# First attention: x in two parts, context laid out turned, mask product in 64x64 pieces

## The chip, the cores and the metric

The kernel runs on one core of a Trainium2 chip. Its engines work side by side, each through its own queue of instructions in order: TensorE (PE, matmuls; PEld, its weight loads), VectorE (DVE), ScalarE (ACT), GpSimd (POOL), and SyncE (SP), which issues most of the loads. They wait for one another with semaphores. The metric is the time of one execution on the device in microseconds (us), lower is better.

## The reference

Four layers, each a gated cross attention and a gated feed-forward block, are applied to x (16 batches of 128 rows of 256 values, float32). The change touches the first attention alone:

```python
x = x + jnp.tanh(g_xattn[0]) * _L0_xattn_ref(_layernorm(x), ctx, ctx, mask, wq, wk, wv, wo, bo)

def _L0_xattn_ref(q, k, v, mask, wq, wk, wv, wo, bo):     # 16 heads of 16 values
    qh, kh, vh = heads(q @ wq), heads(k @ wk), heads(v @ wv)
    scores = einsum('nqha,nkha->nhqk', qh, kh)
    scores = where(mask == 0, -1e10, scores)
    attn = softmax(scores / sqrt(16), axis=-1)
    return einsum('nhqk,nkha->nqha', attn, vh).reshape(N, Lq, 256) @ wo + bo
```

The layer normalisation takes mean and variance over the 256 values of each row of x. ctx is 16 x 128 x 256, the mask 16 x 1 x 128 x 128 of int32.

## The kernel before, in words

All of x stays in on-chip memory for the whole program. The first stage is `narrow_attention` (L291), one pass over the 16 batches, written out by hand for every engine; the later stages are not touched.

**Start.** `Prologue` (L178) holds the loads and the statistics that come before the loop. SyncE issues four loads of x (`on_sync`, L189, four batches of 512 KB in each), then ctx and mask of batches 0 and 1, then wq, wk, wv, wo and the bias bo (L334 to L342). VectorE takes `bn_stats` of the 16 batches, each four after their load (`on_vector`, L218), waits for the tanh of the gates, and `finish_norm_vector` (L229) turns the statistics into 1/std and -mean/std in a chain of eight small operations, with a square root on ScalarE (`finish_norm_scalar`, L258) in the middle. TensorE meanwhile runs ten `stay_warm` products (L265, two matmuls each) on the identity.

**A batch.** `front` (L386) has three fillings of one PSUM bank: T turns the normalised x (L393) and ctx (L396) with two transposes each, and ScalarE evicts the four as one tile xcT (L512); QK makes Q and K from it in 16 matmuls (L402), V makes V in 4 (L407). `scores` (L411) first writes the additive mask into four score banks, each by one matmul of a 128x128 bf16 identity against the mask repeated for four heads (512 columns, L418), and then adds the scores of the 16 heads, 32 matmuls with tiles of 32 rows (L425). VectorE (`shift`, L589) takes the row maximum of each bank (L593) and subtracts it (L597); ScalarE takes the exponential (L534); TensorE turns the probabilities (`transposed`, L435); `weighted` multiplies them with V and with ones (L449, tiles of 32 columns); VectorE divides (L604, L608); `project` multiplies with wo (L458), and VectorE adds the result into x and takes its statistics (L615, L284). `weigh` (L583) makes the additive mask of a batch from the int32 mask (L586).

**Order.** Each engine's `body` runs one batch and takes in parts of its neighbours: TensorE does scores of batch b, the last turning of b-1, the projection of b-2, QK of b+1, the weighted sum of b-1, V of b+1, three turnings of b, T of b+2. `over_batches` (L53) writes out the first two and the last two bodies and loops over pairs of the others, with one branch a pair. Waits in the loop compare a semaphore with a count worked out in a register. SyncE loads ctx and mask of batch b when T of b-2 is filled and the mask of b-2 is used (L346 to L350). GpSimd adds the gated bias to x (L376).

## Time and profile before

| | |
|---|---|
| median of 3 runs | 1626.53 us (1624.03 to 1630.96) |
| span of the profiled execution, first to last instruction | 1600.8 us |
| median less that span | 25.7 us |
| mean granted TensorE clock over the span | 0.923 of full |
| TensorE busy, matmuls / weight loads | 1386.6 us (87%) / 1150.0 us (72%) |
| VectorE, ScalarE, GpSimd busy | 953.2, 664.8, 422.6 us |
| first attention, up to the first instruction of the next stage | 195.8 us |

The profile is of one execution. Times in it are in us from the start of the span. "Idle before" is the time for which the engine stood still before an instruction, and behind the arrow stands what ended it; "issue" means that it waited for nothing that the profile shows. The granted clock is the share of TensorE's full 2.4 GHz that the chip allows in a stretch; its lower level is 0.50.

### The profile page before, as it was taken

How to read it: one execution, taken by the hardware profiler on the slowest of the kernel's cores; microseconds unless marked ns; L12 is line 12 of the kernel's file. 1: busy time of each engine (PE TensorE's matmuls, PEld its weight loads, DVE VectorE, ACT ScalarE, POOL GpSimd, SP SyncE). 2: the span in 40 equal slices, each digit the busy share in tenths (PEclk: the TensorE clock that was granted, in tenths of full speed). 3: DMA queues.
4: the chain of work that ended last, by engine and by line, in shares of the span. 5: the costliest groups of instructions: out<-in, count | busy, mean ns of one | idle time of the engine just before them, and what ended most of it. 6: DMA issues, size and time to landing. Idle time of an engine off the chain costs nothing. (4 is left out here: it accounts for less than half of the span.)

```text
span 1600.8 us, 31601 instructions
## 1 busy us (share of the span) xinstructions
PE 1386.6 (87%) x10662; PEld 1150.0 (72%) x10662; DVE 953.2 (60%) x2331; ACT 664.8 (42%) x1313; POOL 422.6 (26%) x578
## 2 busy tenths in 40 slices
PE   8999878889999994999999998999999997401588
PEld 5888645677799983788888887779999996400245
DVE  4888665666422225777777774832222265688887
ACT  3666453420344430333333334335555522430277
POOL 1000000012122210122221221246666633421141
PEclk9999999899799997999999998889999999755799
DMA  3000020673111107111111202012333344421001
GB/s 107 21 20 15 6 92 1 218 268 61 60 34 41 34 22 226 62 51 49 49 47 32 44 1 93 1 52 92 92 93 93 86 173 134 108 19 10 1 14 40
DMA packets 105328, 106.53 MB, mean 67 GB/s; under 512 B 36080, under 2 KB 92160, under 8 KB 105088
## 3 DMA queue, kind: packets, MB, share of 16 engines
q1 hardware_dynamic: 89312, 70.91, 14.6%
q0 software_dynamic: 11136, 28.93, 6.6%
q10 hardware_dynamic: 4768, 5.25, 1.1%
q8 instruction: 64, 1.05, 0.3%
q14 instruction: 48, 0.39, 0.1%
HBM read 83.19 MB, written 20.71 MB: 65 GB/s over the span
## 5 line engine op out<-in xcount | busy, mean ns | idle before, releaser
L3598 PEld LDWEIGHTS L2f_bank<-L2f_xT,L2f_w_tile 128*128 128x128 f32 x1264 | 154.5, 193 | 7.4 <-ACT L2f_xT L3662 3.4
L3598 PE MATMUL L2f_bank<-L2f_xT,L2f_w_tile 128*128 128x128 f32 x1264 | 155.2, 276 | 3.0 <-ACT L2f_xT L3662 3.0
L785 POOL TENSOR_TENSOR L2x_probs<-L2x_probs,L2x_inv_sum 128x512 f32<-128x512 f32 x64 | 66.3, 1057 | 268.4 <-DVE L2x_inv_sum L1062 268.4
L3712 DVE TENSOR_TENSOR L2f_hT<-L2f_gate_h,L2f_bank 128x256 f32<-128x256 f32 x79 | 33.3, 421 | 148.5 <-ACT L2f_gate_h L3669 148.5
L3521 POOL DMA_INDIRECT L2f_y_rows<-L2f_xn,L2f_put_row x79 | 78.2, 989 | 55.2 <-DVE L2f_xn L3728 51.6
L3656 ACT COPY L2f_w_tile<-L2f_w_up 128x1024 f32 x79 | 82.7, 1046 | 17.4 <-issue 17.4
L3513 POOL DMA_INDIRECT L2f_rows<-L2f_x_rows,L2f_take_row x79 | 77.0, 975 | 44.7 <-DVE L2f_take_row L3496 21.3
L3598 PEld LDWEIGHTS L1f_bank<-L1f_xT,L1f_w_tile 128*128 128x128 f32 x736 | 85.6, 192 | 1.1
L3598 PE MATMUL L1f_bank<-L1f_xT,L1f_w_tile 128*128 128x128 f32 x736 | 85.9, 275 | 0.0
L3615 PE MATMUL L1f_bank<-L1f_w_down,L1f_hT 128*128 x368 | 83.1, 379 | 0.0
L3615 PE MATMUL L2f_bank<-L2f_w_down,L2f_hT 128*128 x316 | 81.4, 380 | 0.1
L3615 PEld LDWEIGHTS L1f_bank<-L1f_w_down,L1f_hT 128*128 128x128 f32 x368 | 68.2, 190 | 8.4
L3573 DVE TENSOR_SCALAR L1f_hT<-L1f_bank,expert_b 128x128 f32<-128x128 f32 x92 | 25.9, 344 | 77.6 <-PE L1f_bank L3598 77.6
L829 PE MATMUL L2x_bank<-L2x_wv,L2x_xcT 128*128 128x512 f32 x128 | 63.3, 617 | 2.4 <-issue 1.0
L836 PE MATMUL L2x_bank<-L2x_xcT,L2x_wq 128*128 128x128 f32 x512 | 62.6, 275 | 1.8 <-DMA L2x_wq<-in_L_xattn_Wq 1.8
L836 PE MATMUL L2x_bank<-L2x_xcT,L2x_wk 128*128 128x128 f32 x512 | 62.5, 275 | 1.3 <-DMA L2x_wk<-in_L_xattn_Wk 1.3
L836 PEld LDWEIGHTS L2x_bank<-L2x_xcT,L2x_wq 128*128 128x128 f32 x512 | 60.8, 192 | 3.6 <-DMA L2x_wq<-in_L_xattn_Wq 2.6
L3571 ACT ACTIVATE L1f_hT<-L1f_bank,expert_b 128x128 f32<-128x128 f32 x92 | 26.4, 368 | 88.3 <-PE L1f_bank L3598 88.3
L3290 PEld LDWEIGHTS L2f_bank<-L2f_xT_all,sh_gu 128*128 128x128 f32 x512 | 61.4, 197 | 0.7
L3669 ACT ACTIVATE L2f_gate_h<-L2f_bank 128x256 f32<-128x256 f32 x79 | 30.3, 384 | 75.6 <-PE L2f_bank L3598 75.6
L3290 PE MATMUL L2f_bank<-L2f_xT_all,sh_gu 128*128 128x128 f32 x512 | 61.4, 280 | 0.0
L836 PEld LDWEIGHTS L2x_bank<-L2x_xcT,L2x_wk 128*128 128x128 f32 x512 | 59.7, 192 | 2.1 <-DMA L2x_wk<-in_L_xattn_Wk 2.1
(677 smaller groups left out, 3321.2 us busy)
## 6 DMA issues: line engine op xcount, KB each, us to landing
L1f_w_up<-in_L_ffn_w SPq DMA_DIRECT2D x16, 512.0 KB, 8.2
L1f_w_down<-in_L_ffn_w SPq DMA_DIRECT2D x16, 512.0 KB, 9.0
L2f_got<-L2f_y_rows SPq DMA_DIRECT2D x16, 512.0 KB, 4.4
L2f_w_up<-in_L_ffn_gate_w SPq DMA_DIRECT2D x16, 256.0 KB, 2.9
L2f_w_up<-in_L_ffn_up_w SPq DMA_DIRECT2D x16, 256.0 KB, 3.0
L2f_w_down<-in_L_ffn_down_w SPq DMA_DIRECT2D x16, 256.0 KB, 3.6
x<-in_x SPq DMA_DIRECT2D x4, 512.0 KB, 7.9
L0x_ctx<-in_ctx SPq DMA_DIRECT2D x16, 128.0 KB, 2.1
```

Source lines behind the costliest of these rows:

```text
L785: nc.gpsimd.tensor_tensor(probs[c][:, :, :], probs[c][:, :, :], inv_sum[:, c, :][:, :, None].to_broadcast([P, 4, P]), ALU.mult).then_inc(s ...
L829: last = nc.tensor.matmul(dst[:, :], xcT[j][:, KT + k, :], wv[:, k, half * 512:(half + 1) * 512], start=(k == 0), stop=(k == KT - 1))
L836: last = nc.tensor.matmul(dst[:, i * P:(i + 1) * P], w[:, k, t * P:(t + 1) * P], xcT[j][:, of + k, :], start=(k == 0), stop=(k == KT - 1))
L3290: t = nc.tensor.matmul(bank[2 + 2 * j + u][:, f * P:(f + 1) * P], sh_gu[:, u, k, f * P:(f + 1) * P], xT_of(b)[:, k * P:(k + 1) * P], start ...
L3513: pool.indirect_dma_start(out=rows[t % 4][:, :], out_offset=None, in_=x_dram[:, :], in_offset=bass.IndirectOffsetOnAxis(ap=take_row[:, t:t ...
L3521: pool.indirect_dma_start(out=y_dram[:, :], out_offset=bass.IndirectOffsetOnAxis(ap=put_row[:, t:t + 1], axis=0), in_=y[t % 4][:, :], in_o ...
L3571: x = nc.scalar.activation(dst, products(j, m), ACT.Relu, bias=bias_col)
L3598: x = nc.tensor.matmul(products(j, m), w_tile[j][:, at:at + P], xT[j][:, k * P:(k + 1) * P], start=(k == 0), stop=(k == KT - 1))
L3615: x = nc.tensor.matmul(bank[6 + j][:, 0:D], hT[j][:, k * P:(k + 1) * P], cols(w_down, e * (FT * D) + k * D, D), start=(k == 0), stop=(k == ...
L3656: nc.scalar.copy(w_tile[j][:, 0:KT * UP], cols(w_up, e * (KT * UP), KT * UP)).then_inc(q["w_tile"], 1)
L3669: nc.scalar.activation(gate_h[j][:, 0:F], bank[2 + j][:, 0:F], ACT.Silu).then_inc(q["silu"], 1)
L3712: nc.vector.tensor_tensor(hT[j][:, 0:F], gate_h[j][:, 0:F], bank[2 + j][:, F:2 * F], ALU.mult).then_inc(q["h"], 1)
```

## The change

- **x in two parts.** SyncE loads the first chunk of x (batches 0 to 3), then wq, wk, the inputs of batch 0, wv, the other three chunks, the inputs of batch 1, wo. VectorE takes the statistics of batches 0 to 3 and finishes their normalisation, makes the first two normalised tiles and the first mask, and does the same for batches 4 to 15 before the second mask. `finish_norm_vector` and `finish_norm_scalar` run twice, on a range of batches. ScalarE takes the tanh of the gates behind the second square root, loads the bias through its own queue, and VectorE makes the gated bias at the end of its first body.
- **Context turned.** The host passes ctx a second time, with each batch transposed into two 128x128 tiles. SyncE loads those; T turns only x, and its eviction is of 256 columns. The wait for ctx moves from T to QK, and SyncE's wait from T of b-2 to V of b-2.
- **Mask product in pieces.** The int32 mask of a batch is loaded twice, into the two halves of the partitions (two loads of 64 partitions), and `weigh` makes 256 columns of it. For two banks at a time, TensorE waits for both, increments a semaphore of its own (`settle`), and writes four pieces, each a 64x64 part of the identity against 512 columns: two halves of a bank's partitions for each of the two halves of the array's rows, each half of the rows into a bank of its own. Eight pieces take the place of four matmuls.
- Seven warming products instead of ten.

```diff
-            prologue.on_sync(sp)
-            for b in range(2):
-                load_inputs(b, b)
-            for n in ("wq", "wk", "wv", "wo"):
-                sp.dma_start(w[n][:, :, :], ins[L0_X[n]].rearrange("(k p) n -> p k n", p=P)
-                             ).then_inc(s["w_" + n[1]], 16)
-            sp.dma_start(bo[:, :], ins[L0_X["bo"]].rearrange("(a n) -> a n", a=1).to_broadcast([P, D])
-                         ).then_inc(s["w_o"], 16)
+            prologue.load_x(sp, (0,))
+            load_weight("wq")
+            load_weight("wk")
+            load_inputs(0, 0)
+            load_weight("wv")
+            prologue.load_x(sp, (1, 2, 3))
+            load_inputs(1, 1)
+            load_weight("wo")
             def body(j, b):
 
-                sp.wait_ge(s["filled"], (b - 2) * NF + (T + 1))
+                sp.wait_ge(s["filled"], (b - 2) * NF + (V + 1))
...
             def load_inputs(j, b):
-                sp.dma_start(ctx_in[j][:, :], one(ins["ctx_1024"], b)).then_inc(s[f"ctx_in{j}"], 16)
-                sp.dma_start(mask_in[j][:, :], one(ins["mask_Bx1xSxS2_ik1"].rearrange("b a q k -> b (a q) k"), b)
-                             ).then_inc(s[f"mask_in{j}"], 16)
+                sp.dma_start(ctxT[j][:, :, :].rearrange("p t c -> p (t c)"), one(ins["ctx_turned"], b)
+                             ).then_inc(s[f"ctxT{j}"], 16)
+                for r in range(MS):
+                    sp.dma_start(mask_in[j][r * MW:(r + 1) * MW, :, :],
+                                 one(ins["mask_Bx1xSxS2_ik1"].rearrange("b a q k -> b (a q) k"), b
+                                     ).rearrange("(c p) k -> p c k", p=MW)).then_inc(s[f"mask_in{j}"], 16)
...
                 if f == T:
 
                     pe.wait_ge(s["xn"], b + 1)
-                    pe.wait_ge(s[f"ctx_in{j}"], loads(b, j))
                     for k in range(KT):
-                        nc.tensor.transpose(front_bank[:, k * P:(k + 1) * P], xn[j][:, k * P:(k + 1) * P],
-                                            core.ident[:, :])
-                    for k in range(KT):
-                        last = nc.tensor.transpose(front_bank[:, (KT + k) * P:(KT + k + 1) * P],
-                                                   ctx_in[j][:, k * P:(k + 1) * P], core.ident[:, :])
+                        last = nc.tensor.transpose(front_bank[:, k * P:(k + 1) * P], xn[j][:, k * P:(k + 1) * P],
+                                                   core.ident[:, :])
                 elif f == QK:
-                    for n, of, at in (("wq", 0, 0), ("wk", KT, D)):
+
+                    pe.wait_ge(s[f"ctxT{j}"], loads(b, j))
+                    for n, of, at in (("wq", xT, 0), ("wk", ctxT, D)):
...
-                for i in range(4):
-
-                    after(pe, s["shifted"], b * 4 + (i - 3))
-                    nc.tensor.matmul(score_bank[i][:, :].rearrange("p (h k) -> p h k", h=4), mask_diag[:, :],
-                                     mask_add[j][:, None, :].to_broadcast([P, 4, P]), start=True, stop=False)
+                for i0 in range(0, 4, MS):
+
+                    after(pe, s["shifted"], b * 4 + (i0 + MS - 4))
+                    settle(pe, s["pe_passed"])
+                    for c in range(MS):
+                        for r in range(MS):
+                            rows = slice(r * MW, (r + 1) * MW)
+                            nc.tensor.matmul(score_bank[i0 + r][c * MW:(c + 1) * MW, :
+                                                                ].rearrange("p (h k) -> p h k", h=4),
+                                             mask_diag[rows, rows],
+                                             mask_add[j][rows, c, None, :].to_broadcast([MW, 4, P]),
+                                             start=True, stop=False)
...
-            stay_warm(core, out_bank, 10)
+            stay_warm(core, out_bank, 7)
...
-            prologue.on_scalar(act)
-            finish_norm_scalar(core, act, s, temps)
+            prologue.load_gates(act)
+            act.dma_start(bo[:, :], ins[L0_X["bo"]].rearrange("(a n) -> a n", a=1).to_broadcast([P, D])
+                          ).then_inc(s["b_o"], 16)
+            nc.scalar.preload_act_table(ACT.Sqrt)
+            finish_norm_scalar(core, act, s, temps, 0, FIRST)
             take(0, 0, T)
...
             take(0, 0, V)
             take(1, 1, T)
+            finish_norm_scalar(core, act, s, temps, FIRST, B, before=1)
+            prologue.squash_gates(act)
             over_batches(act, body)
...
                 if not two_left(b):
                     weigh(j, b + 2)
+                if first:
+
+                    dve.wait_ge(prologue.sems["gates"], 1)
+                    dve.wait_ge(s["b_o"], 16)
+                    nc.vector.tensor_scalar(gated_bias[:, :], bo[:, :], core.gate(layer, 0), None, ALU.mult
+                                            ).then_inc(s["gated_bias"], 1)
...
-            prologue.on_vector(dve)
-            dve.wait_ge(prologue.sems["gates"], 1)
-            finish_norm_vector(core, dve, s, temps)
+            prologue.stats(dve, 0, FIRST)
+            finish_norm_vector(core, dve, s, temps, 0, FIRST)
             norm(0, 0)
             norm(1, 1)
             weigh(0, 0)
+            prologue.stats(dve, FIRST, B)
+            finish_norm_vector(core, dve, s, temps, FIRST, B, before=1)
             weigh(1, 1)
-
-            dve.wait_ge(s["w_o"], 32)
-            nc.vector.tensor_scalar(gated_bias[:, :], bo[:, :], core.gate(layer, 0), None, ALU.mult
-                                    ).then_inc(s["gated_bias"], 1)
```

## Rows read from the trace of the kernel before

**Rows 1.** Busy time by stretch: PE, PEld, DVE, ACT, POOL, granted clock, DMA share, GB/s.

```profile
12.62:15.38 2.76, 0.01 (x1) 0.03 (x1) 2.43 (x13) 0.22 (x1) 0.00 (x0) 1.00 0.74 239
...
16.78:20.18 3.40, 3.40 (x16) 3.21 (x16) 0.07 (x1) 0.00 (x0) 2.02 (x3) 0.57 0.22 58
20.18:23.21 3.03, 1.10 (x5) 0.68 (x5) 0.00 (x0) 1.54 (x5) 0.00 (x0) 0.98 0.00 0
23.21:25.96 2.75, 2.75 (x8) 1.31 (x8) 0.00 (x0) 1.58 (x2) 0.00 (x0) 0.50 0.08 24
...
80.00:100.00 20.00, 19.92 (x288) 16.69 (x286) 17.27 (x29) 12.54 (x28) 1.45 (x2) 1.00 0.06 20
```

**Rows 2.** Timeline 0 to 40: start, duration, engine, line, operation, tiles [idle before].

```profile
7.19 1.41 DVE L223 BATCH_NORM_STATS2 stats<-x 128x6 f32<-128x256 f32 x4 [5.33 <-DMA x<-in_x]
...
8.77 4.43 DVE L223 BATCH_NORM_STATS2 stats<-x 128x6 f32<-128x256 f32 x12 [0.16 <-DMA x<-in_x]
...
11.18 0.19 PEld L270 LDWEIGHTS L0x_bank<-ident 128*128 128x128 f32 x1 [0.24 <-issue]
11.61 0.19 PEld L270 LDWEIGHTS L0x_bank<-ident 128*128 128x128 f32 x1 [0.24 <-issue]
13.23 0.19 DVE L237 TENSOR_TENSOR L0x_temps<-stats 128x16 f32<-128x16 f32 x1
...
14.71 0.74 DVE L279 TENSOR_SCALAR L0x_xn<-x,rstd,neg_mean_rstd 128x256 f32<-128x256 f32 x2
...
15.38 0.41 PE L393 MATMUL L0x_bank<-ident,L0x_xn 128*128 128x128 f32 x2 [2.76 <-DVE L0x_xn L279]
...
16.05 0.59 ACT L512 COPY L0x_xcT<-L0x_bank 128x512 f32<-128x512 f32 x1 [1.87 <-PE L0x_bank L396]
...
21.02 0.37 ACT L520 COPY L0x_kT<-L0x_bank 128x256 f32<-128x256 f32 x1
...
27.40 0.69 DVE L593 TENSOR_REDUCE L0x_top<-L0x_bank 128x4 f32<-128x512 f32 x1 [10.54 <-PE L0x_bank L425]
```

**Rows 3.** Issue of wk in the same timeline; then the loads: size, us to landing.

```profile
7.81 0.65 SPq L339 DMA_DIRECT2D L0x_wk<-in_L_xattn_wk  x1
...
L0x_wk<-in_L_xattn_wk SPq DMA_DIRECT2D x1, 256.0 KB, 6.6
```

**Rows 4.** Timeline of TensorE in the loop (PEld: its weight loads).

```profile
82.84 1.03 PE L418 MATMUL L0x_bank<-L0x_mask_add,L0x_mask_diag 128*128 128x512 bf16 x4
...
92.66 0.38 PE L396 MATMUL L0x_bank<-ident,L0x_ctx 128*128 128x128 f32 x2
92.88 1.03 PE L418 MATMUL L0x_bank<-L0x_mask_add,L0x_mask_diag 128*128 128x512 bf16 x4
93.84 1.17 PE L425 MATMUL L0x_bank<-L0x_kT,L0x_qT 32*128 32x128 f32 x32
...
103.17 0.55 PEld L418 LDWEIGHTS L0x_bank<-L0x_mask_add,L0x_mask_diag 128*128 128x128 bf16 x4 [0.34 <-issue]
```

**Rows 5.** Timeline of VectorE in the same stretch.

```profile
93.64 0.21 DVE L586 TENSOR_SCALAR L0x_mask_add<-L0x_mask 128x128 bf16<-128x128 int32 x1
93.88 0.41 DVE L279 TENSOR_SCALAR L0x_xn<-x,rstd,neg_mean_rstd 128x256 f32 x1
95.03 0.69 DVE L593 TENSOR_REDUCE L0x_top<-L0x_bank 128x4 f32<-128x512 f32 x1 [0.73 <-PE L0x_bank L425]
```

**Rows 6.** Timeline of TensorE in the third attention, where tiles of half size stand.

```profile
740.19 1.95 PE L836 MATMUL L2x_bank<-L2x_xcT,L2x_wq 128*128 128x128 f32 x16
741.97 1.95 PE L836 MATMUL L2x_bank<-L2x_xcT,L2x_wk 128*128 128x128 f32 x16
...
745.95 1.09 PE L875 MATMUL L2x_bank<-L2x_probsT,L2x_v 128*64 128x128 f32 x16
746.97 1.16 PE L847 MATMUL L2x_bank<-L2x_kT,L2x_qT 64*128 64x128 f32 x16
748.06 1.98 PE L829 MATMUL L2x_bank<-L2x_wv,L2x_xcT 128*128 128x512 f32 x4
```

More of the change, by code:

```diff
@@ L188, in __init__, with load_x @@
                                                                                    "cleared"])
-    def on_sync(self, sp):
+    def load_x(self, sp, chunks):
         core = self.core
-        for i in range(B // self.CHUNK):
+        for i in chunks:
             b = i * self.CHUNK
@@ L216, in on_gpsimd, with stats @@
                                      ).then_inc(s["cleared"], 1)
-    def on_vector(self, dve):
-        for b in range(B):
+    def stats(self, dve, lo, hi):
+        for b in range(lo, hi):
             if b % self.CHUNK == 0:
@@ L224, in on_vector, with finish_norm_vector @@
                                          ).then_inc(self.sems["stats"], 1)
-        dve.wait_ge(self.sems["stats"], B)
-def finish_norm_vector(core, dve, s, temps):
+        dve.wait_ge(self.sems["stats"], hi)
+NORM_STEPS = 7
+def finish_norm_vector(core, dve, s, temps, lo=0, hi=B, before=0):
     nc = core.nc
-    st = core.stats[:, :].rearrange("p (b k) -> p b k", k=6)
+    done = before * NORM_STEPS
+    st = core.stats[:, 6 * lo:6 * hi].rearrange("p (b k) -> p b k", k=6)
     mean_e, var_e, mean_o, var_o = st[:, :, 1], st[:, :, 2], st[:, :, 4], st[:, :, 5]
-    half, var, mean, root = (temps[:, k, :] for k in range(4))
+    half, var, mean, root = (temps[:, k, lo:hi] for k in range(4))
@@ L247, in finish_norm_vector @@
     nc.vector.tensor_tensor(var, half, var, ALU.add).then_inc(s["norm_var"], 1)
     nc.vector.tensor_tensor(mean, mean_e, mean_o, ALU.add).then_inc(s["norm_step"], 1)
-    dve.wait_ge(s["norm_root"], 1)
-    nc.vector.reciprocal(core.rstd[:, :], root).then_inc(s["norm_step"], 1)
-    dve.wait_ge(s["norm_step"], 6)
-    nc.vector.scalar_tensor_tensor(core.neg_mean_rstd[:, :], mean, -0.5, core.rstd[:, :], ALU.mult, ALU.mult
+    dve.wait_ge(s["norm_root"], before + 1)
+    nc.vector.reciprocal(core.rstd[:, lo:hi], root).then_inc(s["norm_step"], 1)
@@ L255, in finish_norm_vector, with finish_norm_scalar @@
+    dve.wait_ge(s["norm_step"], done + 6)
+    nc.vector.scalar_tensor_tensor(core.neg_mean_rstd[:, lo:hi], mean, -0.5, core.rstd[:, lo:hi], ALU.mult, ALU.mult
                                    ).then_inc(s["norm_step"], 1)
-    dve.wait_ge(s["norm_step"], 7)
-def finish_norm_scalar(core, act, s, temps):
-    act.wait_ge(s["norm_var"], 1)
-    core.nc.scalar.activation(temps[:, 3, :], temps[:, 1, :], ACT.Sqrt).then_inc(s["norm_root"], 1)
+    dve.wait_ge(s["norm_step"], done + 7)
+def finish_norm_scalar(core, act, s, temps, lo=0, hi=B, before=0):
+    act.wait_ge(s["norm_var"], before + 1)
+    core.nc.scalar.activation(temps[:, 3, lo:hi], temps[:, 1, lo:hi], ACT.Sqrt).then_inc(s["norm_root"], 1)
@@ L294, in narrow_attention @@
     NF = 3
+    MS = 2
+    MW = P // MS
     with ExitStack() as ctx:
@@ L303, in narrow_attention @@
         ones32 = sb(f"{tag}_ones32", [P, 2, 32])
-        ctx_in = [sb(f"{tag}_ctx{j}", [P, D]) for j in range(2)]
-        mask_in = [sb(f"{tag}_mask{j}", [P, P], I32) for j in range(2)]
-        mask_add = [sb(f"{tag}_mask_add{j}", [P, P], BF16) for j in range(2)]
+        ctxT = [sb(f"{tag}_ctxT{j}", [P, KT, P]) for j in range(2)]
+        mask_in = [sb(f"{tag}_mask{j}", [P, MS, P], I32) for j in range(2)]
+        mask_add = [sb(f"{tag}_mask_add{j}", [P, MS, P], BF16) for j in range(2)]
         xn = [sb(f"{tag}_xn{j}", [P, D]) for j in range(2)]
-        xcT = [sb(f"{tag}_xcT{j}", [P, 2 * KT, P]) for j in range(2)]
+        xT = [sb(f"{tag}_xT{j}", [P, KT, P]) for j in range(2)]
         qT = [sb(f"{tag}_qT{j}", [P, 2, KT, P]) for j in range(2)]
@@ L582, in weigh @@
             def weigh(j, b):
-                dve.wait_ge(s[f"mask_in{j}"], loads(b, j))
+                dve.wait_ge(s[f"mask_in{j}"], mask_loads(b, j))
                 after(dve, s["scores"], 4 * (b - 1))
-                nc.vector.tensor_scalar(mask_add[j][:, :], mask_in[j][:, :], L0_MASK["compare"], L0_MASK["times"],
+                nc.vector.tensor_scalar(mask_add[j][:, :, :], mask_in[j][:, :, :], L0_MASK["compare"], L0_MASK["times"],
                                         L0_MASK["op"], ALU.mult).then_inc(s["mask_add"], 1)
@@ L3831 @@
     arrays, ins = {}, {}
-    for name in _INS:
-        a = np.ascontiguousarray(inputs[name])
+    turned = np.asarray(inputs["ctx_1024"]).reshape(B, P, KT, P).transpose(0, 3, 2, 1).reshape(B, P, KT * P)
+    for name in _INS + ["ctx_turned"]:
+        a = np.ascontiguousarray(turned if name == "ctx_turned" else inputs[name])
         arrays[f"in_{name}"] = a
```

26 lines of the change are left out of this document (16 added, 10 removed).

## The prediction

> **What bounds the kernel now.** I read the granted clock and the engines' busy shares by stretch first [rows 1], then the order of work from the start of the program to the first softmax [rows 2], the loads behind it [rows 3], and then one turn of the batch loop, TensorE first and VectorE second [rows 4, 5]. The reader is to see two regimes. Up to 27.40 us the kernel is a chain: every engine waits for the one before, and its first link is all of x. In the loop (from the second batch on) TensorE is busy for 19.92 of 20 us and VectorE for 17.27 [rows 1], so TensorE sets the pace. The mask products of two batches stand 10.04 us apart (82.84 to 92.88), across the loop's branch 10.3 us (92.88 to 103.17) [rows 4]. What is left to VectorE is the idle before its first reduction, 0.73 us a batch [rows 5].
>
> **The start.** Before, VectorE takes 16 statistics, from 7.19 until 13.2, then the chain of small operations (13.23 to 14.71, 1.48 us), then the normalised tile of batch 0, and TensorE turns it at 15.38, 0.67 us after 14.71 [rows 2]. After, the first part needs only the four statistics of the first chunk (1.41 us in the same row). The small operations get four columns instead of sixteen, which I take as the same 1.48 us, since they are far below a tile's work. So: 7.19 + 1.41 + 0.03 + 1.48 + 0.67 = 10.78 instead of 15.38.
> From there link by link. Turning x and evicting it took 1.40 us (15.38 to 16.78, where the first Q product starts [rows 1, 2]). Two of the four transposes go (0.22 us, the distance from the turning of ctx to the mask product in [rows 4]) and the eviction is of 256 columns, not 512 (0.37 against 0.59 us [rows 2]): 0.96, to 11.74. The 16 products of Q and K took 3.40 us at a granted clock of 0.57 [rows 1]; 16 of the same shape at full clock take 1.78 us (740.19 to 741.97) [rows 6], with the tail 1.95: to 13.69. From there to the second batch's turning it was 3.03 us at a clock of 0.98, all of it evictions and the product V: to 16.72. Then turning, mask product and scores, 23.21 to 27.40, 4.19 us with the clock at 0.50 for most of it. At full clock they would be 0.27, about 0.65 (below) and 1.19 (93.84 to 95.03 [rows 4, 5]), together 2.1; at half clock some 2.9 with the shorter mask. I take 2.5 in the middle: the first reduction at 19.2 instead of 27.40, a gain of 8.2 us.
> **The clock.** It stood at 0.50 after two stretches of little work: TensorE idle from 12.62 to 15.38, then 1.10 busy of 3.03 us [rows 1]. These are the 2.4 and the 1.2 GHz levels. Seven warming products instead of ten end six matmuls of 0.43 us earlier [rows 2], at 12.62 - 2.6 = 10.0, so the first gap shrinks from 2.76 to 0.7 us; the later one (evictions of Q and K) stays. So Q and K should run fast and a stretch behind them may not. Where it falls into the first loop body, the 16 products of Q and K there cost up to 1.6 us more. I take 0.7 off: **start 7.5 us**, bounds 4.5 (Q and K at half clock, 1.5; mask, scores and first body at half clock, 1.5) and 9.2 (all at full clock, and x a little sooner since less is queued behind it).
> **What moved behind it.** SyncE's queue now has wq, wk, the first inputs and wv ahead of x's chunks 1 to 3. The loads drain as one stream: wk, issued at 7.81, landed 6.6 us later at 14.4 with 2944 KB in front of and in it [rows 3]. After the change wk ends at 1024 KB, where x's second chunk ended (its statistics start at 8.77 [rows 2]), far ahead of 11.74. The last chunk of x ends at 3008 KB, so about 14.6. Its four statistics (1.4) bring VectorE to 16.0, the small operations to about 17.5, but their square root stands on ScalarE behind the eviction of the second batch's turned x (about 17.4), so they end near 18.3 and the second mask (0.35) at 18.65. The scores arrive at 19.2: hidden, with 0.5 us to spare. The tanh of the gates now stands on ScalarE behind that root: a table load of 1.28 us, perhaps a second one before the first exponential, which is due at 19.2 + 1.4 = 20.6. The Trainium skill, ScalarE: Activation LUTs, lists tanh in the set of exp, by which the second load would be absent and nothing is due; no row here shows the pair, and the price otherwise is 0.3 us. The bias load goes to ScalarE's queue, one issue while that engine has nothing to do. The gated bias (0.35 us) goes to the end of VectorE's first body, ahead of 2 us of idle; GpSimd's first additions wait for it, and their first reader is two bodies later.
>
> **The loop.** (a) The turning of ctx goes, 2 matmuls, 0.22 us of TensorE (92.66 to 92.88) [rows 4]. But its cover goes too: at the branch TensorE's queue sat idle 0.34 us before the mask product with nothing left to wait for [rows 4], so there the issuing of instructions is what is late, and the transposes hid part of that. One wait moves out of this place (ctx) and a semaphore increment comes in (twice). I count 0.13 in a body without the branch, 0 in one with it: 0.07 on average.
> (b) The mask product is now 0.96 us from its start to the scores (92.88 to 93.84): four streams of 0.216 (0.86) and 0.10 of bubble, which also stands before other changes of tile size. Eight pieces of 64x64, each of 512 columns still, in two groups of four. No 64x64 piece is in the trace. The nearest rows are pieces of 64 rows by 128 columns and 128 rows by 64 columns: 16 of them in 1.09 and 1.02 us (746.97 to 748.06, 745.95 to 746.97), where 16 of 128x128 take 1.78 [rows 6]. So pieces of two halves of the rows run side by side, and pieces of two halves of the columns too. If both hold at once, four run together: 2 x 0.216 = 0.43, the bubble behind 0.10, a new bubble ahead 0.10, and 0.05 for the second group's weights. That is 0.68, a gain of 0.28. Bounds: 0.35 if the new bubbles are hidden by issuing; a loss of 0.96 if no two of the eight overlap (8 x 0.216 = 1.73, with bubbles 1.93).
> The Trainium skill, TensorEngine Tiling (Array Packing), Key Properties, says that a change of tiling mode drains the engine. The rows agree in kind, 0.10 us before the scores; by it one more change a batch is due, and the sum has it in.
> (c) VectorE makes the mask additive for 256 columns instead of 128: 0.21 us becomes about 0.35, taken between it and the 0.41 of the 256-column operation behind it [rows 5]. Its slack of 0.73 becomes 0.59, more than TensorE wins, so it stays hidden; 0.59 a batch is the most that the loop can give. ScalarE's shorter eviction and SyncE's third issue a batch are off the path: the inputs are asked for two batches ahead.
> Loop: 0.07 + 0.28 = 0.35 a batch, times 15, and 0.28 for the last: **5.5 us**; bounds 9.2 (0.59 each) and a loss of 14.
>
> **Sum.** 7.5 + 5.5 = 13.0 us. The profiled span is 1600.8, the median of the runs 1626.53, so 25.7 lie around the span and do not change. The span goes to about 1588, the time to **1613.5 us**, 0.8% faster. What follows the stage is not touched; it starts earlier, and its clock may switch at other places: 3 us either way, about the distance of the runs shown.
>
> **The rivals.**
> 1. Four pieces do not run together, only pairs (chance 0.14). For it: no row has rows and columns halved together. Against it: each half works alone [rows 6]. Mask 4 x 0.216 + 0.25 = 1.11, a loss of 0.15; loop -0.08 x 16, a loss of 1.3. Time 1626.5 - 6.2 = 1620.
> 2. The start gains little: x's later chunks or the clock hold up the first softmax (0.15). Gain 3 there: 1618.
> 3. **The other side.** The eight pieces run one after the other, each group held by its own increment on TensorE's queue (0.05). The mask takes 1.93 us or, with 0.2 us more for each of the two increments, 2.33: 0.96 to 1.37 more, less 0.07, times 16 = 14 to 21 us, against 7.5 at the start: 1633 to 1640. It decides once the phase before the scores is over 0.5 us longer than now. The rows of halved tiles speak against it.
> 4. Rivals 1 and 2 together (0.05): 1625.
> A rule of the Trainium skill, TensorEngine Tiling (Array Packing), Gotcha 1, is that different row tiles can't use one PSUM bank at once. Here a group's two row halves go to two banks, so it would not force rival 3; the rows of 64 rows each have two banks as well.
>
> **Chances.** Forecast (both gains, 1607 to 1618) 0.61; the rivals as above. A measurement of this kernel can tell about 0.5%, 8.1 us, from no change, so the line is at 1618.4. Faster: 0.58 of the forecast and some 0.10 of rival 2 and 1, 0.68. Same: 0.24. Slower: rival 3 and an unlucky clock, 0.08. The range reaches from the forecast with the loop's ceiling, 1606, to rival 4, 1625.
>
> **What would show it.** In the profile after: the first transpose near 10.8 us and the first reduction near 19.2; starts of neighbouring mask products 9.65 us apart in place of 10.04; mask start to scores start 0.68 us; VectorE's idle before its first reduction 0.2 to 0.3 us. Wrong would be a mask phase over 1 us, a first reduction after 22 us, VectorE without idle, or a later stage that takes back what this one gave.

## The result, and the profile after

The changed kernel takes 1611.51 us (median of 4 runs, 1608.04 to 1620.17), the kernel before 1628.74 (4 runs, 1624.03 to 1631.17): a ratio of 0.9892, interval 0.9858 to 0.9926, some 17 us or 1.1% faster. A second comparison (11 below) gave 0.9895, interval 0.9865 to 0.9925. The forecast was 1613.5 in a range of 1606 to 1625.

The timeline of the changed kernel's start, in the columns of [rows 2]:

```profile
7.31 1.41 DVE L225 BATCH_NORM_STATS2 stats<-x 128x6 f32<-128x256 f32 x4 [5.45 <-DMA x<-in_x]
...
10.63 0.41 PE L411 MATMUL L0x_bank<-ident,L0x_xn 128*128 128x128 f32 x2 [1.21 <-DVE L0x_xn L285]
...
11.07 0.37 ACT L536 COPY L0x_xT<-L0x_bank 128x256 f32<-128x256 f32 x1 [1.45 <-PE L0x_bank L411]
...
11.70 1.13 PE L419 MATMUL L0x_bank<-L0x_xT,L0x_wq 128*128 128x128 f32 x8 [0.66 <-ACT L0x_xT L536]
...
13.83 0.84 ACT L542 ACTIVATE L0x_qT<-L0x_bank,L0x_parity 128x256 f32<-128x256 f32 x2 [2.38 <-PE L0x_bank L419]
...
16.01 1.41 DVE L225 BATCH_NORM_STATS2 stats<-x 128x6 f32<-128x256 f32 x4 [0.26 <-DMA x<-in_x]
...
16.75 0.44 PE L411 MATMUL L0x_bank<-ident,L0x_xn 128*128 128x128 f32 x2 [0.58 <-ACT L0x_v L550]
...
17.68 0.63 PE L439 MATMUL L0x_bank<-L0x_mask_add,L0x_mask_diag 64*64 64x512 bf16 x8 [0.49 <-ACT L0x_xT L536]
...
18.24 1.17 PE L449 MATMUL L0x_bank<-L0x_kT,L0x_qT 32*128 32x128 f32 x32
18.39 1.28 ACT L208 ACT_TABLE_LOAD   x1
...
19.09 0.41 DVE L285 TENSOR_SCALAR L0x_xn<-x,rstd,neg_mean_rstd 128x256 f32<-128x256 f32 x1
...
19.43 0.69 DVE L622 TENSOR_REDUCE L0x_top<-L0x_bank 128x4 f32<-128x512 f32 x1
...
20.88 0.63 ACT L558 ACTIVATE L0x_probs<-L0x_shifted 128x512 f32<-128x512 f32 x1 [0.98 <-DVE L0x_shifted L626]
```

The chain is read as before: first transpose 10.63 instead of 15.38, first Q product 11.70 instead of 16.78, first reduction 19.43 instead of 27.40. The reduction carries no idle in front: VectorE was at work on its normalised tile until then (19.09), and 19.43 is also 1.19 us after the start of the scores, as in the loop: the two are level. Only one table load stands between the second root and the first exponential.

The loop, TensorE first, then VectorE (answers to [rows 4, 5]):

```profile
72.34 0.63 PE L439 MATMUL L0x_bank<-L0x_mask_add,L0x_mask_diag 64*64 64x512 bf16 x8 [0.34 <-issue]
...
81.47 0.38 PE L411 MATMUL L0x_bank<-ident,L0x_xn 128*128 128x128 f32 x2
81.78 0.63 PE L439 MATMUL L0x_bank<-L0x_mask_add,L0x_mask_diag 64*64 64x512 bf16 x8
82.34 1.17 PE L449 MATMUL L0x_bank<-L0x_kT,L0x_qT 32*128 32x128 f32 x32
...
91.66 0.63 PE L439 MATMUL L0x_bank<-L0x_mask_add,L0x_mask_diag 64*64 64x512 bf16 x8 [0.36 <-issue]
...
82.72 0.28 DVE L615 TENSOR_SCALAR L0x_mask_add<-L0x_mask 128x256 bf16<-128x256 int32 x1
82.98 0.41 DVE L285 TENSOR_SCALAR L0x_xn<-x,rstd,neg_mean_rstd 128x256 f32 x1
83.53 0.69 DVE L622 TENSOR_REDUCE L0x_top<-L0x_bank 128x4 f32<-128x512 f32 x1
```

Mask products stand 9.44 us apart (72.34 to 81.78) and, across the branch, 9.88 (81.78 to 91.66), where they stood 10.04 and 10.3 us apart. The mask now takes 0.56 us to the scores (81.78 to 82.34), not 0.96. The wait for issuing at the branch is still there, 0.36 us, and VectorE's idle before its reduction has shrunk from 0.73 to 0.14 us (83.39 to 83.53), too short for the view to name.

Busy time by stretch, the columns of [rows 1]:

```profile
10.00:20.00 10.00, 6.29 (x69) 4.87 (x70) 7.45 (x27) 3.98 (x10) 0.00 (x0) 1.00 0.78 227
...
80.00:100.00 20.00, 19.64 (x297) 16.82 (x297) 18.36 (x30) 12.77 (x30) 1.46 (x2) 1.00 0.09 26
```

The clock was granted in full from 10 to 20 us, where before it fell to half between 16 and 20 us (0.57 over the products of Q and K) and again from 23 to 26 [rows 1]. VectorE is at 18.36 of 20 us in the loop, TensorE at 19.64.

The next stage's first product stands at 180.6 us, before at 195.9: 15.3 us. Of these 8.0 are the start, 6.8 the loop (mask product of batch 1 to that of batch 15: 133.45 us, before 140.27), 0.5 the rest.

The stretch behind the last mask product needs a warning, since it moves from run to run by more than most of the effects below. It took 22.1 us in the changed kernel, 22.5 before, but 19.5 in the run of experiment 9, with the same work. The same stretch of both, from 10 us behind that product on:

```profile
168.47:174.47 6.00, 5.02 (x60) 4.16 (x64) 1.16 (x3) 1.41 (x2) 0.00 (x0) 0.51 0.01 3
```

```profile
167.57:173.57 6.00, 5.00 (x72) 3.07 (x72) 3.01 (x5) 1.41 (x2) 0.00 (x0) 1.00 0.01 3
```

In the first the granted clock is 0.51, in the second (experiment 9) 1.00. So the start of the next stage carries up to 2.6 us of the clock's doing, and the place of the last mask product is the better mark of what a change did to start and loop.

### The profile page after: what moved, and what is told of

Its sections match the earlier page's. It is cut to its first block and busy times, and to the rows that moved or that the text cites. A ratio compares the mean times of both kernels' runs of the same rounds, so it can differ in the third digit from the quotient of the medians.

```text
span 1618.5 us, 31703 instructions
## 1 busy us (share of the span) xinstructions
PE 1384.5 (86%) x10688; PEld 1144.8 (71%) x10688; DVE 950.0 (59%) x2339; ACT 656.0 (41%) x1313; POOL 421.4 (26%) x578
## 3 DMA queue, kind: packets, MB, share of 16 engines
q1 hardware_dynamic: 91472, 71.83, 14.9%
## 5 line engine op out<-in xcount | busy, mean ns | idle before, releaser
L3545 POOL DMA_INDIRECT L2f_rows<-L2f_x_rows,L2f_take_row x79 | 76.8, 972 | 44.8 <-issue 22.1
L3647 PEld LDWEIGHTS L1f_bank<-L1f_w_down,L1f_hT 128*128 128x128 f32 x368 | 68.2, 190 | 8.4
L3647 PEld LDWEIGHTS L2f_bank<-L2f_w_down,L2f_hT 128*128 128x128 f32 x316 | 53.8, 190 | 28.7 <-issue 24.5
```

Of the source, the lines that this page charges most:

```text
L3545: pool.indirect_dma_start(out=rows[t % 4][:, :], out_offset=None, in_=x_dram[:, :], in_offset=bass.IndirectOffsetOnAxis(ap=take_row[:, t:t ...
L3647: x = nc.tensor.matmul(bank[6 + j][:, 0:D], hT[j][:, k * P:(k + 1) * P], cols(w_down, e * (FT * D) + k * D, D), start=(k == 0), stop=(k == ...
```

## The experiments

Twelve runs followed, 1 to 10 timed once each, with device times between 1612.8 (2) and 1629.6 us (5). Single times of before lay between 1624.8 and 1635.3 us beside them, so a difference of some microseconds is read from the traces and not from these times. This table holds what is read from each one's timeline in the first attention; distances in the loop are between starts of neighbouring mask products, "1 to 15" is from the mask product of batch 1 to that of batch 15, "last part" from there to the next stage.

| kernel | first transpose | first reduction | body / with branch | mask to scores | 1 to 15 | last part | next stage |
|---|---|---|---|---|---|---|---|
| before | 15.38 | 27.40 | 10.03 / 10.28 | 0.96 | 140.3 | 22.5 | 195.9 |
| before, again (5) | 15.29 | 27.93 | 10.03 / 10.28 | 0.96 | 140.3 | 19.9 | 193.8 |
| changed | 10.63 | 19.43 | 9.45 / 9.87 | 0.56 | 133.5 | 22.1 | 180.6 |
| changed, again (11) | 10.70 | 19.07 | 9.45 / 9.87 | 0.56 | 133.5 | 22.1 | 180.3 |
| 1 start undone | 14.94 | 26.06 | 9.45 / 9.87 | 0.56 | 133.4 | 20.8 | 185.8 |
| 2 context undone | 9.89 | 19.35 | 9.71 / 9.99 | 0.56 | 136.0 | 20.8 | 181.9 |
| 3 mask pieces undone | 10.02 | 20.15 | 9.77 / 10.19 | 0.96 | 137.8 | 19.9 | 183.4 |
| 4 pieces in one half of the rows | 10.64 | 19.28 | 9.87 / 10.32 | 0.98 | 139.5 | 22.6 | 186.9 |
| 6 increments doubled | 10.03 | 20.32 | 9.60 / 10.08 | 0.64 | 136.1 | 22.1 | 185.5 |
| 7 all of x first | 9.80 | 24.25 | 9.45 / 9.87 | 0.56 | 133.5 | 19.5 | 183.1 |
| 8 first part of two batches | 9.41 | 17.86 | 9.45 / 9.88 | 0.56 | 133.5 | 19.5 | 176.5 |
| 9 waits ahead, no increments | 10.16 | 20.15 | 9.45 / 9.54 | 0.56 | 131.6 | 19.5 | 177.1 |
| 10 masks made by GpSimd | 9.80 | 18.91 | 9.45 / 9.87 | 0.56 | 133.5 | 19.5 | 177.4 |
| 12 all together | 8.16 | 19.01 | 9.45 / 9.54 | 0.56 | 131.7 | 22.1 | 178.7 |

**1. The start undone.**

```diff
-            prologue.load_x(sp, (0,))
...
+            prologue.load_x(sp, (0, 1, 2, 3))
+            load_inputs(0, 0)
+            load_inputs(1, 1)
...
-            prologue.stats(dve, 0, FIRST)
-            finish_norm_vector(core, dve, s, temps, 0, FIRST)
+            prologue.stats(dve, 0, B)
+            finish_norm_vector(core, dve, s, temps)
```

> The changed kernel with its start undone: x in one part and ahead of everything, ten warming products; turned context and mask pieces stay. Theory (the start is worth 8 us by itself, because the statistics of twelve batches, 5 us, leave the chain and Q and K come out at full clock): the first reduction of VectorE moves from 19.4 back to about 26 us, bodies stay 9.45 and 9.88 us apart, the stage ends 7 to 8 us later than 180.6. Rival (what the start wins is given back in the loop, which is bound by VectorE and would run the same anyway): the stage ends less than 4 us later.

The first reduction fell back to 26.06, as expected, and the loop did not move at all (133.4 us): nothing that the start wins is given back there. The stage ended 5.2 us later, less than the 7 to 8 expected; the 6.6 us of the start are whole up to the last mask product, and the last part, from there to the next stage, was 1.4 us shorter in this profile than in the changed kernel's (20.8 against 22.1), where the clock fell for longer. Its start ran at half clock where the changed kernel's did not; the scores' start and the reduction show it, 2.0 us apart against 1.2:

```profile
24.07 1.96 PE L448 MATMUL L0x_bank<-L0x_kT,L0x_qT 32*128 32x128 f32 x32
...
26.06 0.69 DVE L618 TENSOR_REDUCE L0x_top<-L0x_bank 128x4 f32<-128x512 f32 x1 [8.65 <-PE L0x_bank L448]
```

**2. The context turned on the chip again.**

```diff
+                    for k in range(KT):
+                        last = nc.tensor.transpose(front_bank[:, (KT + k) * P:(KT + k + 1) * P],
+                                                   ctx_in[j][:, k * P:(k + 1) * P], core.ident[:, :])
```

> The changed kernel with ctx turned on TensorE again and the eviction of 512 columns; start and mask pieces as changed. Theory (the transposes partly hid the issuing of the mask product's instructions): a body without the branch 0.1 to 0.2 us longer than 9.45, a body with it up to 0.1 longer than 9.88, the start 0.4 later, the stage 2 to 2.5 us longer. Rival (TensorE's time counts in full): 0.22 in every body, the stage 3.7 us longer. Rival (VectorE is the bound now): no change in the bodies without the branch, the stage 0.5 us longer.

```profile
82.52 0.43 PE L411 MATMUL L0x_bank<-ident,L0x_xn 128*128 128x128 f32 x2
82.78 0.38 PE L414 MATMUL L0x_bank<-ident,L0x_ctx 128*128 128x128 f32 x2
83.09 0.63 PE L440 MATMUL L0x_bank<-L0x_mask_add,L0x_mask_diag 64*64 64x512 bf16 x8
...
93.08 0.63 PE L440 MATMUL L0x_bank<-L0x_mask_add,L0x_mask_diag 64*64 64x512 bf16 x8 [0.21 <-issue]
```

A body without the branch is 0.26 us longer: the turning of ctx starts 0.26 us behind that of x (82.52 to 82.78), and from there to the mask product it is the same 0.31 us as from the turning of x in the changed kernel. With the branch it is 0.12, and there the wait for issuing has shrunk from 0.36 to 0.21 us: the transposes hid a part of it. So TensorE's time counts in full without the branch, as the first rival has it and more than the theory's 0.1 to 0.2, and in part with it, as the theory has it. VectorE did not cap it. Over the loop it is 2.5 us. The next stage stood only 1.3 us later, because the last part was 1.4 us shorter here; up to the last mask product the run was 2.7 us behind the changed kernel (161.13 against 158.47).

**3. The mask product in four matmuls again.**

```diff
-    MS = 2
+    MS = 1
...
-                    settle(pe, s["pe_passed"])
```

> The changed kernel with the mask product as four 128x128 matmuls again, without the increment, and the mask loaded once; start and turned context stay. Theory: mask start to scores start 0.96 instead of 0.56 us, the bubble ahead of it gone (0.09), so a body 0.3 us longer (9.75 and 10.2), the stage 5 us longer. Rival (VectorE binds already in the changed kernel): bodies without the branch 0.1 longer or less, the stage under 3 us longer.

```profile
84.24 1.03 PE L438 MATMUL L0x_bank<-L0x_mask_add,L0x_mask_diag 128*128 128x512 bf16 x4
85.19 1.17 PE L448 MATMUL L0x_bank<-L0x_kT,L0x_qT 32*128 32x128 f32 x32
```

0.32 us in each kind of body, 4.4 us over the loop. With the 2.5 of experiment 2 that is 6.9, and the loop of the change won 6.8: the two parts add. Up to the last mask product this run is 5.0 us behind (163.46 against 158.47), of which 0.6 come from the start, where the clock fell. The next stage stood 2.8 us later, not 5, for the last part took 2.2 us less.

**4. All pieces in one half of the rows.**

```diff
-                    for c in range(MS):
-                        for r in range(MS):
-                            rows = slice(r * MW, (r + 1) * MW)
+                    for r in range(MS):
+                        for c in range(MS):
+                            rows = slice(0, MW)
```

> The changed kernel with all eight pieces in the upper half of the array's rows (the mask loaded and made additive on 64 partitions only), so that pieces can pair over the halves of the columns alone. It computes the same. Theory (a group of four runs together only because it covers both halves of rows and of columns): four streams in a row, mask start to scores start 4 x 0.216 + 0.10 = 0.96 or more, the stage 5 to 6 us longer. Rival (pieces of 64x64 are fast for another reason, as a shorter weight load): 0.56 as before.

```profile
84.17 1.05 PE L439 MATMUL L0x_bank<-L0x_mask_add,L0x_mask_diag 64*64 64x512 bf16 x8
85.15 1.17 PE L449 MATMUL L0x_bank<-L0x_kT,L0x_qT 32*128 32x128 f32 x32
```

The same eight pieces, the same shapes, now 0.98 us: four streams one after the other, two pieces in each. So the 0.56 us of the change come from four pieces at once, one in each quarter of the array. This is also what rival 1 would have cost, 6.1 us over the loop (139.5 against 133.5), which would have eaten nearly all of the loop's gain.

**5. The kernel before once more.**

> The kernel before once more, unchanged, for a second profile. The first profile's span (1600.8 us) stood 25.7 us under the median of its timed runs; the profiles of all changed kernels stand 1.7 us under their own time. Theory (the first profiled execution was itself fast in one later stage, the third layer's routed experts: 372 us there against 400 to 404 in the five other profiles): this profile has about 400 us in that stage, a span near 1627, and the same first attention, 195.9 us to the next stage's first product, first reduction 27.4. Rival (25 us really lie around this kernel's span): span near 1601 again with a time near 1627.

Span 1627.9, time 1629.61. The first reduction came at 27.93, and the next stage at 193.8, not 195.9: the clock stayed up in the last part (19.9 us, not 22.5). One stretch of the third layer's experts, the same 40 us in the first profile of before, in the second, and in that of the changed kernel:

```profile
1137.00:1177.00 40.00, 40.00 (x309) 38.56 (x308) 11.85 (x28) 23.71 (x42) 27.34 (x29) 1.00 0.31 93
```

```profile
1137.00:1177.00 40.00, 35.76 (x262) 32.52 (x261) 9.47 (x24) 19.22 (x35) 23.43 (x25) 1.00 0.25 79
```

```profile
1137.00:1177.00 40.00, 35.61 (x264) 32.76 (x264) 9.39 (x24) 19.44 (x37) 23.40 (x25) 1.00 0.26 79
```

TensorE had 309 matmuls in the first and about 263 in the others. That stage took 372 us in the first profile, 405 here, 399 to 408 in all others. Why one execution ran it 33 us faster is open. What is settled is that the first profile's span can't be set against other profiles, and that 1.7 us (2.2 in run 10), not 25.7, lie around a span.

**6. The increments doubled.**

```diff
                     settle(pe, s["pe_passed"])
+                    settle(pe, s["pe_passed"])
```

> The changed kernel with each increment on TensorE's queue before a group of four pieces doubled. Theory (ahead of the mask product the issuing of instructions is late, so each further queue instruction counts, about 0.1 us each): mask start 0.1 later behind the turning of x, mask start to scores start 0.56 to 0.66, a body 0.1 to 0.2 us longer, the stage 1.5 to 3 us. Rival (the increments are hidden behind running matmuls): nothing changes.

```profile
85.31 0.71 PE L440 MATMUL L0x_bank<-L0x_mask_add,L0x_mask_diag 64*64 64x512 bf16 x8
85.95 1.17 PE L450 MATMUL L0x_bank<-L0x_kT,L0x_qT 32*128 32x128 f32 x32
```

0.64 us instead of 0.56, and a body 0.15 or 0.21 longer: 0.08 to 0.10 for each added increment, one ahead of the product and one in the middle, and 2.6 us over the loop. They are not hidden. That the next stage stands 4.9 us later is not theirs alone: the clock was at 0.50 from 17 to 23 us here.

**7. All of x ahead of the weights.**

```diff
-            prologue.load_x(sp, (0,))
+            prologue.load_x(sp, (0, 1, 2, 3))
             load_weight("wq")
```

> The changed kernel with all four chunks of x loaded ahead of the weights, statistics still in two parts. Theory (the order of the loads is needed as well as the split): wk then ends at 2560 KB in the stream instead of 1024, so about 13 us, and the first Q and K products start at 13.3 instead of 11.7; the second part of the statistics is done earlier; first reduction about 20.9 instead of 19.4. Rival (the split of the statistics alone brings the whole gain): first reduction unchanged at 19.4 or sooner.

```profile
13.70 1.15 PE L418 MATMUL L0x_bank<-L0x_xT,L0x_wq 128*128 128x128 f32 x8 [3.49 <-DMA L0x_ctxT<-in_ctx_turned]
...
17.91 2.04 PE L423 MATMUL L0x_bank<-L0x_wv,L0x_ctxT 128*128 128x256 f32 x4 [1.35 <-ACT L0x_kT L543]
...
15.00:22.00 7.00, 5.07 (x22) 2.91 (x20) 4.38 (x18) 2.26 (x8) 0.00 (x0) 0.50 0.14 37
```

The first Q product waits 3.49 us for its inputs and starts at 13.70, near the 13.3 expected. The reduction came at 24.25, not 20.9: behind that idle the granted clock was 0.50 from 15 to 22 us, and V, mask and scores took up to twice their time. With the start undone altogether (1) it was 26.06, so the split of the statistics alone gave 1.8 of 6.6 us in this run. The late load cost twice here, once as a wait and once with the clock; how much of the second is due to the first is not shown, since the clock also fell in runs without such a wait (3, 6).

**8. A first part of two batches.**

```diff
-    CHUNK = 4
-    FIRST = CHUNK
+    PARTS = [0, 2, 4, 8, 12, 16]
+    FIRST = 2
```

> The changed kernel with a first part of two batches (256 KB) instead of four. Theory A (the start is still bound by the first load and its statistics): first transpose 1.5 to 2 us earlier, first reduction 17.5 to 18. Theory B (the second part is the next bound: its last chunk arrives at 16.0, its statistics, small operations and the second mask keep VectorE until 19.2, just ahead of the scores): first transpose 1.5 to 2 us earlier, but the first reduction at 19.2, 0.2 us won.

```profile
4.85 0.75 DVE L225 BATCH_NORM_STATS2 stats<-x 128x6 f32<-128x256 f32 x2 [2.99 <-DMA x<-in_x]
...
6.94 0.73 DVE L285 TENSOR_SCALAR L0x_xn<-x,rstd,neg_mean_rstd 128x256 f32<-128x256 f32 x2
...
9.41 0.38 PE L411 MATMUL L0x_bank<-ident,L0x_xn 128*128 128x128 f32 x2
...
14.42 1.41 DVE L225 BATCH_NORM_STATS2 stats<-x 128x6 f32<-128x256 f32 x4 [0.23 <-DMA x<-in_x]
...
17.86 0.69 DVE L622 TENSOR_REDUCE L0x_top<-L0x_bank 128x4 f32<-128x512 f32 x1
```

Theory A by the number of the reduction, 17.86; the transpose came only 1.2 us earlier, not 1.5 to 2. Theory B failed in its premise: the last chunk of x was there at 14.42, not 16.0. Its mechanism may still stand, for the reduction follows VectorE's work without idle; but it is also 1.19 us behind the start of the scores (16.67), so VectorE and TensorE are level again, and both follow the loads. And there was more: both normalised tiles were ready by 7.7, but the transpose stood behind the warming products until 9.41.

**9. The waits of the mask product moved ahead.**

```diff
-                pe.wait_ge(s["evicted"], b * NF + (QK + 1))
-                pe.wait_ge(s["mask_add"], b + 1)
...
-                    after(pe, s["shifted"], b * 4 + (i0 + MS - 4))
-                    settle(pe, s["pe_passed"])
...
+                if not last:
+                    pe.wait_ge(s["mask_add"], b + 2)
                 transposed(b, 1)
                 transposed(b, 2)
+                if not last:
+                    pe.wait_ge(s["shifted"], 4 * b + 4)
```

> The changed kernel without the two increments on TensorE's queue: the waits of the mask product (mask ready, last bank of the batch before read) stand ahead of the turning of the probabilities and of x, where the wait for Q's eviction already stood. Theory (each queue instruction right before the mask product costs 0.1 us, since the doubled increments made a body 0.20 us longer): the issuing is no longer late, the wait of 0.34 us at the branch shrinks to 0.1 or less, mask start to scores start 0.53; but VectorE has 0.14 us of idle left in a body without the branch and 0.40 in one with it, so bodies come to 9.35 and 9.5 us, the stage 2 to 3 us shorter. Rival (the bubble ahead of the mask is the change of tile size alone): bodies unchanged, the stage 0 to 0.5 us shorter.

```profile
72.53 0.63 PE L434 MATMUL L0x_bank<-L0x_mask_add,L0x_mask_diag 64*64 64x512 bf16 x8
...
81.98 0.63 PE L434 MATMUL L0x_bank<-L0x_mask_add,L0x_mask_diag 64*64 64x512 bf16 x8
...
83.72 0.69 DVE L622 TENSOR_REDUCE L0x_top<-L0x_bank 128x4 f32<-128x512 f32 x1 [0.15 <-PE L0x_bank L444]
```

Bodies with the branch went from 9.87 to 9.54, those without did not move from 9.45, where 9.35 was expected, and the mask still took 0.56 us. So at the branch the issuing was late, and is no more; in the other body the bubble ahead of the mask (0.09 us) is not the increments', which are hidden there. Each view was right for one kind of body. The run moved the waits and took out the increments together, so their shares in the 0.33 us are not known. It is 1.8 us over the loop; the other 2.6 us by which the next stage stood earlier are the last part at full clock.

**10. The masks made by GpSimd.**

```diff
-                nc.vector.tensor_scalar(mask_add[j][:, :, :], mask_in[j][:, :, :], L0_MASK["compare"], L0_MASK["times"],
+                nc.gpsimd.tensor_scalar(mask_add[j][:, :, :], mask_in[j][:, :, :], L0_MASK["compare"],
```

> The changed kernel with the additive masks of batches 2 to 15 made by GpSimd instead of VectorE, which is 0.28 us a body less for VectorE. Theory (TensorE still sets the pace in the changed kernel, VectorE is just under it): bodies stay 9.45 and 9.88 us apart, VectorE's idle before its first reduction grows by 0.25 to 0.3 us. Rival (VectorE is the bound in the bodies without the branch): those come to 9.2 us, the stage 1.5 us shorter.

```profile
83.00 0.69 DVE L632 TENSOR_REDUCE L0x_top<-L0x_bank 128x4 f32<-128x512 f32 x1 [0.38 <-PE L0x_bank L460]
...
84.32 1.07 POOL L397 TENSOR_SCALAR L0x_mask_add<-L0x_mask 128x256 bf16<-128x256 int32 x1 [8.09 <-DMA L0x_mask<-in_mask_Bx1xSxS_ik]
```

VectorE's idle grew from 0.14 to 0.38 us, which is 0.24 where 0.25 to 0.3 was expected, and the loop kept its 133.5 us. TensorE sets the pace in the changed kernel too, with VectorE close under it.

**11 and 12, timed together.** The changed kernel again, and one with the two-batch part, the waits ahead, no increments and five warming products.

> The changed kernel once more, unchanged, timed in five rounds against the kernel before. Theory (16 to 17 us, of which 15.3 in the first attention by the first pair of profiles, the rest chance in later stages): a ratio of about 0.990, the stage again 9.66 us a body, first reduction between 18.9 and 20.2 depending on when x lands and the clock falls.

1617.07 us (6 runs, 1613.5 to 1618.6) against 1632.37 of before (11 runs): 0.9895, interval 0.9865 to 0.9925. The stage repeated itself to 0.3 us.

```diff
-            stay_warm(core, out_bank, 7)
+            stay_warm(core, out_bank, 5)
```

> The changed kernel with what three runs pointed to together: a first part of two batches, the mask product's waits ahead and no increments, five warming products (in the run with two batches the first transpose stood behind the seventh warming product, at 9.4, with its input ready at 7.4). Theory (the gains add): first transpose 8.2, first reduction 17.5 (the second part of the statistics binds, its last chunk lands near 14.4), bodies 9.45 and 9.54 us, the next stage's first product near 174 instead of 180.6, the time 5 to 6 us under the changed kernel, ratio 0.986. Rival (the shorter warming costs the clock, so the products of Q and K run at half clock): first reduction 19 or later, no gain over the changed kernel at the start, 2.5 us from the loop alone.

```profile
8.16 0.38 PE L411 MATMUL L0x_bank<-ident,L0x_xn 128*128 128x128 f32 x2
...
16.05 0.93 PE L434 MATMUL L0x_bank<-L0x_mask_add,L0x_mask_diag 64*64 64x512 bf16 x8 [1.33 <-DMA L0x_wo<-in_L_xattn_wo]
...
19.01 0.69 DVE L622 TENSOR_REDUCE L0x_top<-L0x_bank 128x4 f32<-128x512 f32 x1 [1.11 <-PE L0x_bank L444]
...
14.50:19.00 4.50, 3.17 (x43) 2.02 (x41) 3.07 (x14) 2.08 (x4) 0.00 (x0) 0.69 0.35 100
```

1614.26 us (6 runs, 1609.11 to 1618.24), 0.9874 of before, interval 0.9842 to 0.9906. It beats the kernel before; whether it beats the changed one these runs can't tell: the medians differ by 2.8 us, not the 5 to 6 expected, and the intervals overlap. The loop kept its gain (131.7). The start did not: the transpose came at 8.16 as expected, but the reduction at 19.01. That is the rival's number but not its reason, for the clock was at 1.00 from 8 to 14 us, over the products of Q and K. TensorE waited 1.33 us for wo, which it needs only two batches later: its wait stands ahead of the loop, and this load, the last in SyncE's queue, is what is late. Behind it the clock was granted at 0.69.

This wait is not new in 12. In 8, 9 and 10 the first mask product waited for wo too, 0.16, 0.33 and 0.81 us:

```profile
17.17 0.63 PE L450 MATMUL L0x_bank<-L0x_mask_add,L0x_mask_diag 64*64 64x512 bf16 x8 [0.81 <-DMA L0x_wo<-in_L_xattn_wo]
```

In the changed kernel wo was issued at 11.27 and took 6.3 us to land, so 17.6, and the mask product started at 17.68 after 0.49 us of idle. The view puts that idle down to the eviction of xT, which ended at the same time, but the program has no wait for it there: what it waits for ahead of the loop is wo. The kernel before had wo at 14.8, long before its first mask product at 24.12. The wait for wo moved behind the first scores was not tried; since VectorE was level with the scores in 8, 10 and the changed kernel, it would have gained there only with VectorE's part earlier as well.

## Why the prediction was right, point by point

- **The start's chain** was right link by link up to the second batch's turning: first transpose 10.78 forecast, 10.63 measured; Q 11.74 and 11.70; the turning 16.72 and 16.75. Q and K ran at full clock. The last link, to the first reduction at 19.2 and 19.43 (19.07 in the second run), agrees in part by luck: 2.5 us stood for it, halfway between 2.1 at full clock and 2.9 at half. It took 2.68 at full clock, since TensorE was idle 0.49 us before its mask product (the late wo), which no term had.
- **The deduction for the clock**, 0.7 us, was not due in either profile of the changed kernel, and it is not settled that it never is: in kernels 3, 6, 9 and 12, with starts only 0.5 to 2.5 us earlier, the clock fell before the first scores, and the first reduction was at 19.0 to 20.3. In 2, 8 and 10, with starts 0.7 to 1.2 us earlier, it did not. What decides it these runs don't show. So the start gave 8.0 where 7.5 stood, with the clock on its side.
- **What moved behind it.** The last chunk of x was put at 14.6 and came at 16.01, so VectorE's second part was not 0.5 us ahead of the scores but level with them; the profile shows no idle in front of the reduction. The step that failed is the load's time of landing, taken from bytes alone. The bytes were also miscounted: the mask is loaded twice, 64 KB more, and the bias, 128 KB, went out at 1.80 through the other queue. But the same count of bytes landed at 15.5 to 15.7 in runs 9, 10 and 11 and at 14.4 in 8 and 12, so bytes do not settle it. The same paragraph left out wo, which the new order puts last: its wait was priced at nothing, and it held the first mask product back in 8, 9, 10, 12 and, by the program's order, in the changed kernel. So behind the first load both the last chunk of x and wo stand next in line.
- **The tanh.** One table load of 1.28 us (18.39) and none before the first exponential (20.88), which waited for VectorE. The 0.3 us for a second load were rightly left out. The Trainium skill, ScalarE: Activation LUTs, Table sets: the hidden batching unit, lists tanh in the set of exp; the trace agrees.
- **The loop, the transposes.** 0.13 and 0 us were counted for the two kinds of body. Experiment 2 shows 0.26 and 0.12. The term stood at 0.07 us on average and is 0.19; the mechanism, that they partly cover the issuing at the branch, is shown by the wait of 0.21 against 0.36 us.
- **The loop, the mask.** 0.68 us forecast, 0.56 measured. Of the 0.12 us, 0.10 are the bubble ahead, which was counted inside this distance but lies before its start: from the turning of x to the mask product it is 0.31 us here (81.47 to 81.78), and 0.22 from the last turning to the mask product before. The gain of the mask alone, 0.28 forecast, is 0.32 by experiment 3. Both terms together, 0.35 a batch, were 0.49: 6.8 us measured where about 5 stood for the same fourteen distances. So the mis-sized term of the loop is mainly the transposes'. The sign "9.65 us apart in place of 10.04" came at 9.44 for the same reason.
- **The ceiling by VectorE** of 0.59 us a body was reached almost exactly in bodies without the branch (10.04 to 9.45), yet experiment 10 shows that it did not hold them; that the two numbers meet is chance. Its mask operation took 0.28 us, not 0.35.
- **The step that was wrong** is the account of the time around the span. With 1.7 us around its span the profiled execution took about 1602.5 us, 24 less than the runs beside it, in a stage that the change does not touch, and I put this down to time outside the span. Since the forecast was made as a difference it went through unharmed. Had it been made as a share of the span, it would have been off.
- **The rivals.** Rival 1 was excluded by experiment 4 (pairs would be 0.98 us), rival 3 with it; rival 2 by the first reduction at 19.4. The increments of rival 3 do cost, 0.08 to 0.10 us each where they were doubled, but 0.2 was too high.
- **The sum.** 13.0 us forecast, 17 measured (interval 12 to 23). Start and loop give 14.9 to 15.8 up to the last mask product, by the two profiles of either kernel (173.38 and 173.95 before, 158.47 and 158.13 after); with the last part, where the clock differs, the stage gives 13.2 to 15.6. The remaining 1 to 4 us are within the interval and in no row; the profiles' time behind the first attention scatters from 1428 to 1439 us (the first profile of before left out), so nothing is claimed for them. The lower end of the range, 1606, is not the loop's ceiling alone (1626.5 - 7.5 - 9.2 is 1609.8); it needs some 3 us from the later stages too.

## What to carry to other kernels

A small product with a stationary operand of many zeros (here a diagonal) can be cut into blocks that sit in different quarters of the array; each block then streams the same columns, but four at once, and the price is one more bubble of 0.09 us and an operand laid out in both halves of the partitions. When part of a chain at the start is cut off, order the loads by first use before splitting the arithmetic: without that order the split gained 1.8 of 6.6 us here. Look also at the load that this order puts last, and at where the program waits for it: here the wait for wo stood ahead of scores that do not need it. And instructions that only wait or count stand in the queue's time wherever the queue has run dry, as at a loop's branch; hoisting the waits ahead of longer work and dropping the increments was worth 0.33 us a branch.

## What the runs showed of the hardware

- Four pieces of 64x64 with 512 bf16 columns run at once, two row halves into two banks and two column halves into one bank: 0.56 us to the next product for eight of them, 0.98 when all eight sit in the same half of the rows and only the column halves differ.
- In experiment 7 TensorE stood idle from 10.2 to 13.7 us, and the granted clock was 0.50 from 15 to 22. At the start of the changed kernel it stayed at 1.00 with gaps of at most 1.35 us, yet it fell in its last part, at 168.5 us, behind 2 us in which TensorE was busy for 0.91. In experiment 9 the same last part stayed at 1.00: the same work met either level.
- The same program's expert stage took 372 us in one execution and 399 to 408 in all the others of this and its sister kernels. One profile is one draw, and its span may be the odd one.
